# Feed-forward stages of a six-stage kernel, worked two batches (512 tokens) a turn

## The reference, cut to what matters

```python
h = jnp.einsum('bsd,hd->bsh', layernorm(x), bw1) + b1     # bw1 = alpha1 * sign(w1), 512 x 128
h = jax.nn.gelu(h, approximate=False)
out = jnp.einsum('bsh,dh->bsd', h, bw2) + b2              # bw2 = alpha2 * sign(w2), 128 x 512
x = x + 0.5 * out
```

## Time before, and the profile before

| | |
|---|---|
| median of 3 executions | 2290.44 us (2286.01 to 2292.85) |
| profiled execution | 2287.4 us, its span 2285.4 us |
| TensorE busy in the span | 2177.7 us (95%) |
| VectorE, ScalarE, GpSimd busy | 1520.7 (67%), 1241.2 (54%), 685.5 us (30%) |
| mean granted TensorE clock | 0.987 of full speed |

### The profile page before, as it was taken

The page is one execution under the profiler, slowest core; times in us unless marked ns, Lnnn a source line. Parts: engine busy times, 40 slices in busy tenths (PEclk is TensorE's granted clock), DMA queues, the critical chain, the costliest instruction groups (busy, mean ns, idle before and its releaser), DMA issues. The chain is left out here.

```text
span 2285.4 us, 42519 instructions
## 1 busy us (share of the span) xinstructions
PE 2177.7 (95%) x13706; PEld 1753.3 (77%) x13706; DVE 1520.7 (67%) x4922; ACT 1241.2 (54%) x2504; POOL 685.5 (30%) x724
## 2 busy tenths in 40 slices
PE   5989998999999999899999999999999899999995
PEld 5978888977777777777677777877777777777775
DVE  6867776866677776556666566666666676777664
ACT  4645445655444554465566665666665444544542
POOL 0412222433575555500000000000100344665545
PEclk9999999999999999999999999999999999999998
DMA  8040000000111111200000000000000011111222
GB/s 275 0 175 0 0 0 1 2 10 23 35 42 41 37 38 47 54 5 0 0 0 0 0 0 1 1 1 1 1 1 1 12 28 40 45 51 50 51 54 73
DMA packets 70648, 68.44 MB, mean 30 GB/s; under 512 B 9312, under 2 KB 57952, under 8 KB 70112
## 3 DMA queue, kind: packets, MB, share of 16 engines
q1 hardware_dynamic: 60960, 47.62, 6.5%
q0 software_dynamic: 8192, 16.79, 3.2%
q10 hardware_dynamic: 1344, 2.16, 0.3%
HBM read 32.47 MB, written 34.08 MB: 29 GB/s over the span
## 5 line engine op out<-in xcount | busy, mean ns | idle before, releaser
L2031 ACT ACTIVATE moe_fc<-moe_bank,all_b_fc 128x380 f32<-128x380 f32 (+2 forms) x448 | 245.8, 549 | 301.4 <-PE moe_bank L1961 298.3
L2138 DVE SCALAR_TENSOR_TENSOR moe_act<-moe_bank,all_b_moe_gate,moe_fc 128x380 f32<-128x380 f32 (+2 forms) x448 | 256.9, 576 | 169.5 <-PE moe_bank L1965 107.1
L1977 PEld LDWEIGHTS moe_bank<-all_w_proj,moe_act 128*128 128x128 f32 x2560 | 300.0, 192 | 12.2 <-issue 2.4
L1977 PE MATMUL moe_bank<-all_w_proj,moe_act 128*128 128x128 f32 x2560 | 305.7, 276 | 2.0 <-DVE moe_expert_out L2147 2.0
L1800 POOL DMA_INDIRECT all_landed<-rows_out,all_take_at x256 | 267.5, 1045 | 117.8 <-issue 114.5
L1494 POOL COPY lin_xn_ones<-lin_xn 128x254 f32<-128x254 f32 x32 | 12.7, 398 | 722.8 <-PE lin_bank L1244 722.4
L1876 POOL TENSOR_SCALAR moe_hot<-all_slot_ids,moe_slot 128x608 fp32r<-128x608 f32 x112 | 202.3, 1814 | 67.6 <-DVE moe_slot L2115 32.8
L2038 ACT ACTIVATE moe_act<-moe_act 128x760 f32<-128x760 f32 (+2 forms) x224 | 174.8, 780 | 85.0 <-DVE moe_act L2138 84.3
L1388 ACT ACTIVATE lin_neg<-lin_bank 128x512 f32<-128x512 f32 x256 | 151.7, 593 | 105.8 <-PE lin_bank L1236 62.1
L1286 PEld LDWEIGHTS lin_bank<-lin_kv,lin_qT 128*128 128x128 f32 x1024 | 145.1, 192 | 74.3 <-issue 62.3
L1961 PE MATMUL moe_bank<-gau_rowsT,all_w_fc 128*128 128x380 f32 (+2 forms) x448 | 171.4, 464 | 1.6 <-ACTq L2042 1.6
(11 more groups left out here) (248 smaller groups left out, 4557.0 us busy)
## 6 DMA issues: line engine op xcount, KB each, us to landing
rows_out<-moe_expert_out SPq DMA_DIRECT2D x96, 128.0 KB
rows_out<-all_zeros SPq DMA_DIRECT2D x1, 9728.0 KB, 28.8
rows_out<-moe_expert_out SPq DMA_DIRECT2D x80, 62.0 KB
all_landed<-rows_out,all_take_at POOLq DMA_INDIRECT x256, 2.8
out<-all_x SPq DMA_DIRECT2D x5, 640.0 KB, 4.5
all_w_fc<-in_w_fc SPq DMA_DIRECT2D x1, 2048.0 KB, 10.0
all_w_gate<-in_w_gate SPq DMA_DIRECT2D x1, 2048.0 KB, 13.9
all_w_proj<-in_w_proj SPq DMA_DIRECT2D x1, 2048.0 KB, 18.5
```

Of the source, the lines that this page charges most:

```text
L1977: last = nc.tensor.matmul(bank[OUT][:, j * DIM:(j + 1) * DIM], act_in[:, i % 2, h, j * P:(j + 1) * P], k.w_proj[:, e * MC + h, :], start=( ...
L2031: nc.scalar.activation(fc[:, j, 0:c.width], bank[FC + j % 2][:, 0:c.width], ACT.Identity, bias=k.b_fc[:, e * MC + j:e * MC + j + 1]).then_ ...
L2138: nc.vector.scalar_tensor_tensor(act_in[:, i % 2, j, 0:c.width], bank[GATE + j % 2][:, 0:c.width], k.b_moe_gate[:, e * MC + j:e * MC + j + ...
```

## The change

A turn takes two batches (`DUO`), four tiles, 512 tokens; there are 16 turns (`TURNS`). `up` is 8 matmuls of 512 columns, one bank for each chunk and one set of banks; each chunk waits for the Gelu of the same chunk of the turn before. Transposed rows fill bank 4, the output bank 5. `xn` has one buffer, the parts and `hT` still two. The loop of `ffn0` on PE and ACT is written out. The routing plan is as it was, and its 33 turns are dealt two to a turn of the stage. The order on PE within a turn is another one.

```diff
-        xn = k.sb("xn", [P, 2, TILES, DIM])
-        parts = k.sb("x_parts", [P, 2, 2, SEQ], F32R)
-        hT = k.sb("hT", [P, 2, FC, SEQ])
+        xn = k.sb("xn", [P, DT, DIM])
+        parts = k.sb("x_parts", [P, 2, 2, DS], F32R)
+        hT = k.sb("hT", [P, 2, FC, DS])
...
-                def bias(b):
+                def bias(p):
...
+                        for s in range(DUO):
+                            routing.on_gpsimd(pool, DUO * p + s)
...
+                def normalise(p):
+                    if p:
+                        dve.wait_ge(xT_ps.sem, xT_ps.at(p - 1))
+                    for t in range(DT):
+                        last = norm.apply(xn[:, t, :], 0, 0, p * DT + t)
+                    last.then_inc(xn_ready.sem, 1)
+                def low_part(p):
+                    dve.wait_ge(high_sb.sem, high_sb.at(p))
+                    nc.vector.tensor_tensor(parts[:, p % 2, 1, :], bank[ROWS_T][:, :], parts[:, p % 2, 0, :], ALU.subtract).then_inc(xT_sb.sem, 1)
...
+                for p in range(2):
+                    normalise(p)
+                    low_part(p)
+                normalise(2)
...
+                for p in range(TURNS):
+                    if p + 3 < TURNS:
+                        normalise(p + 3)
+                    if p + 2 < TURNS:
+                        low_part(p + 2)
+                    beside(DUO * p)
+                    add_out(p)
+                    add_bias(p)
+                    beside(DUO * p + 1)
```

`beside(b)` holds, for the plan's turn b, the pieces of later norms and DVE's share of the routing. On PE and ACT:

```diff
+                def up(p):
+                    pe.wait_ge(xT_sb.sem, xT_sb.at(p))
+                    for c in range(FC):
+                        if p:
+                            pe.wait_ge(h_sb.sem, h_sb.at(p - 1, 0, c))
+                        for j in range(2):
+                            last = nc.tensor.matmul(bank[c][:, :], k.w1T[:, c, :], parts[:, p % 2, j, :], start=(j == 0), stop=(j == 1))
                         last.then_inc(h_ps.sem, 1)
...
-                for b in range(0 if route else BATCHES - 4, BATCHES):
-                    if b + 1 < BATCHES:
-                        up(b, 1, 1 - b % 2)
-                    if b + 3 < BATCHES:
-                        transpose(b, 3, 1 - b % 2)
-                    down(b, b % 2)
+                transpose(0)
+                transpose(1)
+                up(0)
+                for p in range(TURNS):
+                    if p + 2 < TURNS:
+                        transpose(p + 2)
+                    if p + 1 < TURNS:
+                        up(p + 1)
                     if route:
-                        routing.on_tensor(pe, b)
+                        routing.on_tensor(pe, DUO * p)
+                    down(p)
+                    if route:
+                        routing.on_tensor(pe, DUO * p + 1)
...
+                high_part(0)
+                high_part(1)
+                gelu(0)
+                for p in range(TURNS):
+                    if p + 2 < TURNS:
+                        high_part(p + 2)
+                    if p + 1 < TURNS:
+                        gelu(p + 1)
                     if route:
-                        routing.on_scalar(act, b)
-                    if b + 3 < BATCHES:
-                        high_part(b, 3, 1 - b % 2)
+                        routing.on_scalar(act, DUO * p)
+                        routing.on_scalar(act, DUO * p + 1)
```

More of the change, by code:

```diff
@@ L556, in ffn_stage, with rows @@
         last_row = k.sb("wv_last_row", [P, INNER]) if first else None
+        def rows(p):
+            return k.x[:, p * DT:(p + 1) * DT, :]
         with nc.Block() as block:
@@ L693, in up @@
-                def up(b, lag, par):
-                    pe.wait_ge(xT_sb.sem, xT_sb.at(b, lag))
-                    for i in range(2):
-                        pe.wait_ge(h_sb.sem, h_sb.at(b, lag - 2, i))
-                        for c in (2 * i, 2 * i + 1):
-                            for j in range(2):
-                                last = nc.tensor.matmul(bank[2 * par + i][:, (c % 2) * SEQ:(c % 2 + 1) * SEQ],
-                                                        k.w1T[:, c, :], parts[:, par, j, :], start=(j == 0), stop=(j == 1))
-                        last.then_inc(h_ps.sem, 1)
@@ L744, in gelu @@
-                def gelu(b, lag, par):
-                    act.wait_ge(o_ps.sem, o_ps.at(b, lag - 2))
-                    for i in range(2):
-                        act.wait_ge(h_ps.sem, h_ps.at(b, lag, i))
-                        for c in (2 * i, 2 * i + 1):
-                            last = nc.scalar.activation(hT[:, par, c, :], bank[2 * par + i][:, (c % 2) * SEQ:(c % 2 + 1) * SEQ],
-                                                        ACT.Gelu, bias=k.b1[:, c:c + 1], scale=k.alpha[:, c:c + 1])
-                        last.then_inc(h_sb.sem, 1)
@@ L753, in _ @@
-                for b in range(2):
-                    high_part(0, b, b % 2)
-                for i in range(2):
-                    act.wait_ge(h_ps.sem, h_ps.at(0, 0, i))
-                    for c in (2 * i, 2 * i + 1):
-                        last = nc.scalar.activation(hT[:, 0, c, :], bank[i][:, (c % 2) * SEQ:(c % 2 + 1) * SEQ],
-                                                    ACT.Gelu, bias=k.b1[:, c:c + 1], scale=k.alpha[:, c:c + 1])
-                    last.then_inc(h_sb.sem, 1)
@@ L761, in _, with high_part @@
-                high_part(0, 2, 0)
-                if not route:
-                    with act.Fori(0, BATCHES - 4, 2) as b:
-                        for s in range(2):
-                            gelu(b + s, 1, 1 - s)
-                            high_part(b + s, 3, 1 - s)
-                for b in range(0 if route else BATCHES - 4, BATCHES):
-                    if b + 1 < BATCHES:
-                        gelu(b, 1, 1 - b % 2)
+                def high_part(p):
+                    act.wait_ge(xT_ps.sem, xT_ps.at(p))
+                    if p >= 2:
+                        act.wait_ge(h_ps.sem, h_ps.at(p - 2))
+                    nc.scalar.copy(parts[:, p % 2, 0, :], bank[ROWS_T][:, :]).then_inc(high_sb.sem, 1)
@@ new lines, in gelu @@
+                def gelu(p):
+                    if p >= 2:
+                        act.wait_ge(o_ps.sem, o_ps.at(p - 2))
+                    for c in range(FC):
+                        act.wait_ge(h_ps.sem, h_ps.at(p, 0, c))
+                        nc.scalar.activation(hT[:, p % 2, c, :], bank[c][:, :], ACT.Gelu, bias=k.b1[:, c:c + 1],
+                                             scale=k.alpha[:, c:c + 1]).then_inc(h_sb.sem, 1)
+                high_part(0)
+                high_part(1)
```

183 lines of the change are left out of this document (75 added, 108 removed).

## The result

The changed kernel takes 2299.09 us (median of 9 executions, 2296.76 to 2303.95) where the kernel before takes 2288.86 (9 executions, 2285.12 to 2292.85): a ratio of 1.0046, with a 95% interval of 1.0038 to 1.0054. The change makes it slower by 10.2 us; 2299.5 was forecast, 9.1 above a before of 2290.44. The profiled execution took 2297.53 us, its span 2295.7, with a mean clock of 0.985.

The account below looks back on a forecast made before the run. Both stages were taken as bound by TensorE, with a VectorE-slowed stretch in `ffn0`. -6.0 (`ffn0`) + 10.0 (`ffn2`) + 5.1 (clock) = +9.1 us, giving 2299.5 us, range 2287 to 2306.

Parts of the forecast that it names:

- Part 1: Steady turn on TensorE: a 512-column `up` matmul costs 0.216 us, `up` 1.73; first to last `down` 83.4 us.
- rival B: `up` costs 0.238 us a matmul, or the clock rises late in both starts: +4.9 us, 2304.4; chance 0.12.
- Rival D: A 512-column matmul costs no more than one of 256, weight load setting both: 21.7 us less, 2277.8; chance 0.05.
- Part 2: VectorE in a two-batch turn: 4.0 us of 5.7; stalls in 56 to 90 us go, 0.2 us left.
- Part 3: `ffn0` as a whole: -11.4 us between first and last `down`, +3.0 start, +2.4 end, sum -6.0 us.
- Part 4: `ffn2` and its moved routing steps: waits 13.7 us, first to last `down` +4.7, start +3.0, end +2.3; sum +10.0 us.
- The wait of turn 20: `ffn2`: `send0` on TensorE waits 0.8 us for `hot1` on VectorE, behind `choose`.
- that of turn 30: `ffn2`: `send0` waits 3.3 us for VectorE's `add_out`, statistics, norm piece and `hot1`, the last `down` queued behind.
- the two of 0.3 before the route transposes: `ffn2`, turns 8 and 18: route transposes wait 0.3 us each for a normalising now behind `add_out` and statistics.
- Part 5: Clock behind `ffn2`'s waits: of five, three followed by a fall costing 1.7 us each, +5.1 us, between 0 and 8.5.
- A: The clock holds through `ffn2`'s waits, without falls: 2294.4 us; chance 0.30.
- C: `ffn2`'s waits for ScalarE cost nothing, as it serves route steps before TensorE comes: -3.3 us, 2287.1; chance 0.12.

Follow-up runs that it names:

- e5: Kernel before with only the second feed-forward stage (`ffn2`) in turns of two batches: 2301.53 us, ratio 1.0052 to the kernel before.
- e11: Repeat of e5, kernel before with only the second stage in turns of two: 2304.31 us, ratio 1.0065 to the kernel before.
- e2: Changed kernel with ScalarE's route step of the even plan turn placed ahead of the Gelus: 2286.08 us, ratio 0.9990 to the kernel before.
- e9: e2 plus TensorE's routing step of plan turn 30 placed behind the last `down`: 2278.02 us, ratio 0.9961 to the kernel before.
- e6: Changed kernel with each `up` product of 512 columns made as two of 256: 2302.60 us, ratio 1.0061 to the kernel before.
- e8: The changed kernel measured again, nothing altered: 2299.85 us, ratio 1.0046 to the kernel before.
- e3: Changed kernel with seven extra identity products on TensorE ahead of the routing step in four turns: 2294.65 us, ratio 1.0027 to the kernel before.
- e7: Changed kernel with every pair of 512-column `up` products made twice: 2346.85 us, ratio 1.0257 to the kernel before.
- e4: Kernel before with only the first feed-forward stage (`ffn0`) in turns of two batches: 2280.12 us, ratio 0.9955 to the kernel before.
- e1: Changed kernel with both plan turns of TensorE's routing placed behind `down`: 2286.99 us, ratio 0.9987 to the kernel before.
- e10: Repeat of e4, kernel before with only the first stage in turns of two: 2284.57 us, ratio 0.9979 to the kernel before.

## Why the prediction was right, and where it was not

**Part 1, a steady turn: the step that failed in size.** The 0.216 us taken for an `up` matmul, from a plain float32 row of 256 columns, was mis-sized: it is 0.231, with 0.10 us for the change to `down` on top, which the sum left out. The turn is 5.87 us for the forecast 5.73: `up` and the change take 0.22 us more than forecast, the transposes (43.84 to 44.20) 0.06 less. From first to last `down`, `ffn0` took 121.35 - 34.40 = 86.95 us for 84.6: 14 turns by 0.14 are 2.0 of the 2.35. That the excess of `up` over `down` was a cost per matmul was wrong: a pair of 256 columns costs 0.236 us, one of 512 0.231. Twice the cost for twice the columns (rival B's price, 0.238) was nearer. The rule in the Trainium skill, "TensorE: Matmul & The Clock Gate", section "Back-to-back issue gap", with 131 ns for 512 columns in a stream, does not hold for these products of rounded float32: 231 ns measured. Rival D fell with it.

**Part 2, DVE: right.** No stall is left in 56 to 90 us. Where before 2.6 us were idle, PE is busy all through; one small stall of 0.29 us stands at 91.34.

**Part 3, `ffn0`: the sign right, the gain smaller.** Start: first `down` 34.40 - 23.16 = 11.2 us after the first normalising, for 11.8 forecast and 8.8 before, so +2.4 for +3.0. End: 126.75 + 0.87 - 121.35 = 6.3 us for 6.0 forecast, +2.7. In all 104.5 us for 108.4, -3.9 where -6.0 was forecast. Start and end nearly cancel, and part 1 is the difference. The same stage of the kernel before took 1.5 us more in the profiles of e5 and e11 (111.3 for 109.8), because the clock rose one burst later, so against these the gain is 5.4.

**Part 4, the moved steps: right, and the main thing.** Four waits for ACT at the forecast turns: 1.80, 1.74, 1.80 and 2.03, in all 7.4 us for 9.0. A wait was forecast at 2.25, from 2.15 to 4.4 us of the turn; in the first of them the turn starts at 407.68, the last product of `up` ends at 2.45 by its modelled end (408.03 + 2.10) and PE goes on at 4.26. So PE was busy 0.30 us longer than forecast, mostly since the forecast ended `up` at the issue of its last product and not at that product's end (by the costs of part 1, transposes and `up` are issued in 0.35 + 8 x 0.231 = 2.20 us), and ACT was 0.14 quicker. The wait of turn 20 was 0.54 for 0.8, that of turn 30 3.22 for 3.3; the two of 0.3 before the route transposes didn't come. The sum of waits is 11.1 for 13.7. Start 367.70 - 356.45 = 11.2 for 8.7 before (+2.6), end 485.48 + 0.87 - 480.08 = 6.3 for 3.0 (+3.3 for the forecast +2.3; of it 0.86 is the last burst, partly at the low clock). e2 and e9 take the waits away, and with them the stage is back at 115.1 us.

**Part 5, the clock: the mechanism right, the count not.** All five waits, not three, were followed by 0.50, here and in e5, e6 and e8; in e11 three of five were. So the forecast's throw of a coin was right in kind, with odds that were too low. The bursts behind them were longer by 1.72, 1.63, 1.72, 1.53 and 0.86 us, and the two slow `L425` steps, by the distance to the burst behind, by 0.13 and 0.52: 8.1 us for the forecast 5.1. A fall cost 1.6 us where 1.7 was taken. e3 shows it alone: 5.9 us for four.

**The sum.** First to last `down` in `ffn2`: 83.4 + 7.5 for the plain stage and the routing, 2.0 for the steady turns, 11.1 for waits and 7.3 for the falls before the last `down` make 111.3; 480.08 - 367.70 = 112.4 were measured. The stage lost 129.9 - 111.5 = 18.4 us for the forecast 15.1. `ffn0` and `ffn2` together are +14.5 for +9.1. The total is +10.2, since `gau1` came out 4.8 us shorter in this profile, 2.4 in e8's.

**Where the 4.8 us in `gau1` come from.** Its code is unchanged. Windows of its first microseconds before:

```profile
133.00:139.00 6.00, 5.10 (x12) 3.68 (x13) 1.94 (x5) 3.55 (x5) 0.00 (x0) 0.50 0.96 357
140.00:142.00 2.00, 0.59 (x4) 0.21 (x2) 1.31 (x5) 0.97 (x4) 1.11 (x2) 1.00 1.04 391
143.50:146.00 2.50, 2.50 (x7) 1.99 (x6) 1.06 (x3) 1.25 (x3) 0.00 (x0) 0.50 1.04 389
```

and after:

```profile
131.00:133.00 2.00, 2.00 (x5) 1.64 (x6) 0.44 (x2) 1.96 (x3) 0.00 (x0) 0.50 1.03 382
133.70:143.00 9.30, 7.37 (x43) 6.21 (x42) 5.55 (x15) 4.55 (x10) 1.47 (x2) 1.00 1.03 386
```

Before, the clock fell twice as the stage began, and the first time it stayed low through most of the first batch; after, it was up again at 133.7. By what the clock lacked around the entry (the time at 0.50, times one half), the profiles of the thirteen kernels and repeats fall into three kinds. Of the ten with the first stage in turns of two, two lack 1.7 us (`gau1` 227.4 and 227.5 us long), three lack 3.4 (227.7 to 228.3) and five lack 5.1 (229.8 to 230.5). The three with the old first stage lack 5.1 (231.5 to 232.2). So the 4.8 us are mostly a draw of the clock at one entry, which e8 did not repeat. Some 1.5 us that is left at an equal clock has no explanation here, and whether the changed first stage makes the good draws likelier can't be told from three profiles against ten.

The rest, whose code is unchanged too, moves more. By the same measure, without the low stretch at its very end, which all have, its clock lacked 5.1 us in e5 (1802.7 us long), 6.8 in e9 and e7 (both 1803.6), 8.5 to 11.7 in the next five (1804.9 to 1807.0), and 13.7 in e4, e8, e2, e3 and e6 (1808.2 to 1808.8). So e5's profiled execution is 3.4 us shorter than the kernel before's in stages whose code is the same.

**The rivals.** A (the clock holds) did not come, with five falls of five, though two waits of e11 went its way. B was half right: its price for `up`, 0.238, was nearly met, with 2.0 us a stage. C (ACT gets to the copies first) did not occur by itself, but is what e2 makes by hand: -13 us. D is out by e6 and e7. The forecast's mechanism held and its total was 0.4 us off; against the sum by stages, +14.5 for +9.1, it was too kind. A slip of counting in the prediction changes nothing: D, half of C and less than half of B are at most 0.17 left out of the range, not 0.18.

## What to carry to other kernels

When the order of work on an engine is changed, walk through every step that stands in its list and ask which engine's step of the same turn it needs and what that engine has ahead of it; here one call on ScalarE placed behind four Gelus cost 13 us, more than the change could gain. A wait on TensorE can be paid twice: in its length, and in the clock behind it (1.5 us for each in e3, behind 20 of 22 waits of 1.7 to 2.0 us in `ffn2`). Moving the waiting step can hand the wait to another engine, as in e1. Doubling the columns of a product saves little where cost goes by columns (0.231 us for 512, 0.236 for two of 256), so ask first what is paid per instruction, and set against it the longer start and end of a pipeline with larger turns (5 to 6 us a stage here).

## What the runs showed of the hardware that had not been expected

- Behind 20 of 22 waits of TensorE of 1.71 to 2.03 us inside `ffn2` (four each in the changed kernel, e5, e6, e8 and e11, two in e1) the granted clock was 0.50; so it was behind all eight of 3.21 and 3.22 us, and behind none of the four of 1.07 to 1.13 us in e7 (the bursts there took 3.82 us and less). The two without a fall are those of e11, 1.80 and 1.74 us. The kernel before has two more: 2.00 us in the earlier trace rows, and 1.99 us at 88.72 us in `ffn0`, inside the window at 1.00 of the earlier trace rows. So the length alone does not settle it.
- Fourteen small matmuls whose result nobody reads, in place of most of an idle 1.8 us, four times over, made the kernel faster by 5.2 us (e3).
- One kernel's executions spread over 9 us (e10: 2278.01 to 2287.18), with a mean clock of 0.988 in the short ones and 0.985 in the long. The profiles show at four places how: the entry of `gau1` and the rest (above), the two waits of e11 that had no fall behind them, and the start of `ffn0`, where the first `down` burst of the old stage took 2.05 us in one profile and 3.32 and 3.33 in e5 and e11. Effects of less than 5 us need more executions than five, or the lengths of stages.
